# Last projection of the first layer: half of each sum in three f32r terms, half in fp32

## The chip, the cores and the metric

The kernel runs on one core of one Trainium2 chip. The metric is the device time of one execution in microseconds (us); a kernel's time is the median of its runs. Engine names: PE is TensorE, DVE VectorE, ACT ScalarE, POOL GpSimd, SP SyncE.

## The reference, cut to what matters

Two decoder layers over x of shape (2, 1024, 256), each with self-attention, cross-attention and a feed-forward part. The piece around the change is the end of the first layer and the opening of the second:

```
h = gated_gelu(layernorm(x) @ ff_w1 + ff_b1)   # 2048 tokens x 1024
x = x + h @ ff_w2 + ff_b2                      # 1024 -> 256: the projection that is changed
# second layer
h = layernorm(x) * ln1_w + ln1_b
qkv = h @ qkv_w + qkv_b                        # first slices of it are made in the same stage
```

Everything is float32. The projection is a sum over 1024 rows of ff_w2, that is eight row tiles of 128.

## The kernel before

The 2048 tokens are 16 token tiles of 128. `project_norm` (L2591) is one helper for six projections, named po0, pc0, pf0 (first layer) and po1, pc1, pf1 (second). It runs as a block of its own: all engines enter it together and leave it together. The call that changes is pf0 (L3160). Its input `src` is oT (the trace calls it o), 8 row tiles by 2048 tokens, and its weights are w_out (8 row tiles by 256).

**Groups.** The 16 token tiles go in nine groups: seven of two, then two of one (L2595). For group i:

- TensorE `product(i)` (L2727): for each token tile a sum over the KN = 8 row tiles into PSUM. In fp32 each of the eight products appears in the trace as two instructions (two passes). Then `turn(i - 1)` (L2759), four transposes of normalised rows (two in a single-tile group), then the work that `beside` brings along.
- VectorE `stats_of(i)` (L2789): adds the product to x (L2796), takes statistics and the variance plus eps (L2804, L2808, L2811). Then `normalise(i)` (L2813): a reciprocal and one subtract-and-multiply per token tile (L2822), which waits for ScalarE's square root.
- ScalarE `root(i)` (L2855), then `evacuate(i - 1)` (L2860): the turned rows to hT.
- GpSimd `add_bias` (L2682): the bias onto x, four token tiles at a time, in four instructions (L2686).

**Beside pf0.** `thin_attention` (L85) hands over the opening of the second layer's self-attention. SyncE loads its weights. ScalarE's `clear` (L356) fills q_top and k_top in four 2048-wide instructions, behind the root of group 0. In groups 2 to 9, TensorE makes one part of q/k (L290) and one of v (L298) each, ScalarE and VectorE drain the q/k part (L337, L372), and VectorE drains the v part (L382) behind the group's normalising. GpSimd fills v_buf with ones (L694, `gpsimd_early`) right behind the fourth bias addition, and VectorE's first v drain waits for that (`zeroed`, L377). All four bias additions and the memset stand at the head of GpSimd's queue; it has nothing else in this block.

**Products of parts.** Other calls (po0, pc0, pf1) pass `parts=True`. Then group 0 is still made in fp32, and from group 1 on each sum is 24 f32r products: high half of source times high half of weights, high times low, low times high (L2743). ScalarE makes the high halves (w_hi, once; s_hi per token tile, L2877), VectorE the low half of the weights (L2835) and of even token tiles, GpSimd that of odd token tiles (L2655 in both). s_hi and s_lo are rings of RING = 4 token tiles; ScalarE refills a slot when the product that read it is done (L2880 to L2882). Each engine runs `low_parts` or `high_parts` two groups ahead. With parts, GpSimd's queue has another order (L2704): bias 0, low part of group 1, then for i from 0: a bias addition at i = 0, 2 and 4, and the low part of group i + 2.

```
                if parts:
                    add_bias(0)
                    low_parts(1)
                    for i in range(NG):
                        if i % 2 == 0 and i // 2 + 1 < TT // XCHUNK:
                            add_bias(i // 2 + 1)
                        if i + 2 < NG:
                            low_parts(i + 2)
```

`add_bias(c)` ends in `beside.gpsimd(pool, c)`, so the memset follows the bias addition with c = 3, at i = 4. ScalarE, for each i, runs high_parts(i + 2), root(i), evacuate(i - 1), then beside; VectorE stats_of(i), low_parts(i + 2), normalise(i), then beside.

Of the kernel before, what the change touches and what calls it, by code (L numbers as in the profile page):

```python
# [20 lines left out]
F32 = mybir.dt.float32  # L21
F32R = mybir.dt.float32r
BF16 = mybir.dt.bfloat16
U8 = mybir.dt.uint8
ALU = mybir.AluOpType
ACT = mybir.ActivationFunctionType
AX = mybir.AxisListType

P = 128
B, T, D = 2, 1024, 256  # L30
# [2558 lines left out]


def project_norm(nc, shared, name, src, wts, loads, early, x, ln, hT, ident, out, prefetch=(), x_in=None, x_src=None,  # L2591
                 beside=Beside(), split=None, parts=False, lag=1):

    groups, at = [], 0
    for size in [GROUP] * (TT // GROUP - 1) + [1] * GROUP:  # L2595
# [3 lines left out]
    NG = len(groups)  # L2599
    RING = 2 * GROUP  # L2600
# [3 lines left out]
    with ExitStack() as ctx:  # L2604
        def sb(n, shape, dt=F32):
            return ctx.enter_context(nc.sbuf_tensor(f"{name}_{n}", shape, dt))

        KN = src.shape[1] if src is not None else 0
# [6 lines left out]
        hn = sb("normed", [P, 2, GROUP, D]) if ln else None  # L2615
        if parts:

            w_hi, w_lo = [sb(n, [P, KN, D], F32R) for n in ("w_hi", "w_lo")]
            s_hi, s_lo = [sb(n, [P, RING, KN, P], F32R) for n in ("src_hi", "src_lo")]
        prod = [ctx.enter_context(nc.psum_tensor(f"{name}_prod{i}", [P, GROUP, D], F32)) for i in range(NPROD)]  # L2620
        turned = [ctx.enter_context(nc.psum_tensor(f"{name}_turned{i}", [P, KD, GROUP * P], F32)) for i in range(2)]

# [15 lines left out]
        w_high, w_low = shared["w_high"], shared["w_low"]  # L2638
# [13 lines left out]
        def low_part(engine, j):  # L2652

            at = slice(j * P, (j + 1) * P)
            engine.tensor_tensor(s_lo[:, j % RING], src[:, :, at], s_hi[:, j % RING].bitcast(F32),  # L2655
                                 ALU.subtract).then_inc(src_low[j % 2].sem, 1)

        with nc.Block() as block:  # L2658
# [66 lines left out]
            @block.tensor  # L2725
            def _(pe):
                def product(i):  # L2727
                    first, size = groups[i]
                    if i == 0:
                        pe.wait_ge(loaded.sem, loaded.since(DMA * len(loads)))  # L2730
                    if i >= NPROD:
                        pe.wait_ge(summed.sem, summed.since(i - NPROD + 1))
                    for t in range(size):
                        at = (first + t) * P
                        if parts and i:
                            mm = product_of_parts(i, t, first + t)
                            continue
                        for k in range(KN):
                            mm = pe.matmul(prod[i % NPROD][:, t, :], src[:, k, at:at + P], wt[:, k, :],  # L2739
                                           start=(k == 0), stop=(k == KN - 1))  # L2740
                    mm.then_inc(prod_full.sem, 1)

                def product_of_parts(i, t, j):  # L2743
                    dst, u = prod[i % NPROD][:, t, :], j % RING
                    if i == 1 and t == 0:
                        pe.wait_ge(w_high.sem, w_high.since(1))
                    pe.wait_ge(src_high.sem, src_high.since(j - GROUP + 1))
                    for k in range(KN):
                        pe.matmul(dst, s_hi[:, u, k, :], w_hi[:, k, :], start=(k == 0), stop=False)  # L2749
                    if i == 1 and t == 0:  # L2750
                        pe.wait_ge(w_low.sem, w_low.since(1))
                    for k in range(KN):
                        pe.matmul(dst, s_hi[:, u, k, :], w_lo[:, k, :], start=False, stop=False)  # L2753
                    pe.wait_ge(src_low[j % 2].sem, src_low[j % 2].since((j - GROUP) // 2 + 1))
                    for k in range(KN):
                        mm = pe.matmul(dst, s_lo[:, u, k, :], w_hi[:, k, :], start=False, stop=(k == KN - 1))  # L2756
                    return mm

                def turn(i):  # L2759
                    first, size = groups[i]  # L2760
                    pe.wait_ge(normed.sem, normed.since(i + 1))
                    if i >= 2:
                        pe.wait_ge(h_done.sem, h_done.since(i - 1))
                    for k in range(KD):
                        for t in range(size):
                            mm = pe.transpose(turned[i % 2][:, k, t * P:(t + 1) * P],
                                              hn[:, i % 2, t, k * P:(k + 1) * P], ident[:])
                    mm.then_inc(turn_full.sem, 1)

                def ready(i):  # L2770
                    pe.wait_ge(h_done.sem, h_done.since(i + 1))

                for i in range(NG):
                    if KN:
                        beside.source(pe, groups[i][0])
                        product(i)
                    if ln and i >= lag:
                        turn(i - lag)
                    beside.tensor(pe, i, ready)
                if ln:  # L2780
                    for i in range(NG - lag, NG):
                        turn(i)
                    beside.tensor(pe, NG, ready)

            @block.vector
            def _(dve):
# [45 lines left out]
                beside.ahead(dve)  # L2832
                if parts:
                    dve.wait_ge(w_high.sem, w_high.since(1))
                    dve.tensor_tensor(w_lo[:], wt[:], w_hi[:].bitcast(F32), ALU.subtract).then_inc(w_low.sem, 1)  # L2835
                    low_parts(1)
                ahead = lag - 1 if KN else 1
                for i in range(ahead):
# [15 lines left out]
            def _(act):  # L2854
# [22 lines left out]
                def high_parts(i):  # L2877
                    for j in tiles_of(i):
                        at = slice(j * P, (j + 1) * P)
                        if j >= RING + GROUP:  # L2880
                            pe_at = group_of[j - RING] + 1
                            act.wait_ge(prod_full.sem, prod_full.since(pe_at))  # L2882
                        nc.scalar.activation(s_hi[:, j % RING], src[:, :, at],
                                             ACT.Identity).then_inc(src_high.sem, 1)

                if parts:
                    act.wait_ge(loaded.sem, loaded.since(DMA * len(loads)))
                    nc.scalar.activation(w_hi[:], wt[:], ACT.Identity).then_inc(w_high.sem, 1)
                    high_parts(1)
                for i in range(NG if parts and not ln else 0):  # L2890
                    if i + 2 < NG:
# [191 lines left out]
def decoder_blocks(nc, a, out):  # L3083
# [16 lines left out]
    with ExitStack() as ctx, ExitStack() as thin_ctx:  # L3100
# [28 lines left out]
        with scoped("o0", [P, NG, NT]) as oT:  # L3129
            with scoped("w_out0", [P, NG, D]) as w_out, scoped("bias_out0", [P, D]) as bias_out:  # L3130
# [11 lines left out]
                with scoped("wk0", [P, KC, HEADS * 64]) as wk, scoped("wv0", [P, KC, HEADS * 64]) as wv, \  # L3142
                        scoped("wq0", [P, KD, HEADS * 64]) as wq:
                    fetch_kv = [(wk[0:CW], by_rows(L0["ca_wk"], CW), kv_in[0]), (wv[0:CW], by_rows(L0["ca_wv"], CW), kv_in[0]),
                                (wq[:], by_rows(L0["ca_wq"]), kv_in[0])]
                    kv = {"wk": wk, "wv": wv, "wq": wq, "sem": kv_in[0], "count": len(fetch_kv)}
                    project_norm(nc, norm_sems, "po0", oT, wts, loads, True, x, True, hT, ident, None, fetch_kv, x_in, x_dram,
                                 parts=True)
                    loads = norm_loads(wts, [(w_out[:], by_rows(L0["ca_wo"]))], L0["ca_bo"], (L0["ln3_g"], L0["ln3_b"]))
                    folded_attention(nc, "ca0", hT, ctxT, ident, kv, oT, loads)  # L3150
                with ExitStack() as ff_ctx:
                    split, hidden = hidden_layer(nc, "ff0", ff_ctx, by_rows(L0["ff_w1"]), column(L0["ff_b1"]), True)
                    project_norm(nc, norm_sems, "pc0", oT, wts, loads, True, x, True, hT, ident, None, split=split,
                                 parts=True)
                    loads = norm_loads(wts, [(w_out[:], by_rows(L0["ff_w2"]))], L0["ff_b2"], (L1["ln1_w"], L1["ln1_b"]))
                    hidden(oT, loads)
                early, run, finish = thin_attention(nc, "sa1", thin_ctx, hT, ident, key_low, a["causal_rows"],
                                                    {"qkv": by_rows(L1["qkv_w"]), "bias": column(L1["qkv_b"]),
                                                     "bias_row": row(L1["qkv_b"])})
                project_norm(nc, norm_sems, "pf0", oT, wts, loads, True, x, True, hT, ident, None, beside=early)  # L3160

        thin = {"G": 4, "dh": 16, "biased": True}
        NG = HEADS // 4
# [32 lines left out]
        with scoped("w_out2", [P, 4 * D // P, D]) as w_out, scoped("bias_out2", [P, D]) as bias_out, \  # L3196
                scoped("hid1", [P, 4 * D // P, NT]) as hid:
            wts = {"w": w_out, "bias": bias_out, "ln": lns}
            loads = norm_loads(wts, [(w_out[:], by_rows(L1["mlp2_w"]))], L1["mlp2_b"], None)
            hidden(hid, loads)  # L3200
            ff_ctx.close()
            project_norm(nc, norm_sems, "pf1", hid, wts, loads, True, x, False, hT, ident, out_dram, parts=True)


def causal_rows():
# [32 lines left out]
```

## Time and profile before

| | |
|---|---|
| median of 3 runs | 1787.26 us (1785.79 to 1788.02) |
| profiled execution, its own time | 1787.46 us |
| its span, first to last instruction | 1785.7 us |
| PE busy over the span | 1633.4 us, 91% |
| DVE, ACT, POOL busy | 64%, 59%, 54% |
| mean granted TensorE clock | 0.975 |
| the stage pf0 | about 1128.7 to 1210.4 us |

Busy time is that of instructions of one engine, overlaps counted once. The granted clock is the share of TensorE's full 2.4 GHz that the chip gives; it is 1.00 or 0.50, and a number between is a mean over a stretch with both. In a timeline each row is a run of instructions of one kind on one engine, and the idle time in front of them stands in brackets with what ended it; LDWEIGHTS (PEld) overlaps the products. A wait for several things is put down to the one that came last.

### The profile page before, as it was taken

To read this page: it belongs to the slowest core of one execution; us is meant where nothing else is said; L and a number is where in the kernel's file an instruction comes from. 1 tells how busy PE (TensorE), PEld (TensorE's weight loads), DVE (VectorE), ACT (ScalarE), POOL (GpSimd) and SP (SyncE) were. 2 spreads that over 40 slices of the span, in tenths; PEclk is the share of its full clock that TensorE was granted. 3 is DMA by queue.
4 is the path that set the end of the run, shared out by engine and by line. 5 is a ranking of instruction groups with operands and counts; after the bars stand their busy time and mean duration, and the time that the engine had idled before them with its cause. 6 is when DMAs were issued, how large, how long until landed. Compare 5 with 4: busy or idle time off the path is not lost. (4 is left out here: it accounts for less than half of the span.)

```text
span 1785.7 us, 28486 instructions
## 1 busy us (share of the span) xinstructions
PE 1633.4 (91%) x9748; PEld 1046.9 (59%) x9748; DVE 1141.7 (64%) x1985; ACT 1060.8 (59%) x1376; POOL 962.2 (54%) x734
## 2 busy tenths in 40 slices
PE   6889999999999999988998989996989888898799
PEld 4445545444444444378787978884445436565579
DVE  7557677777777777476775933347787845776513
ACT  4556688888888888833556433311767772454452
POOL 1456688888888888952233710202334444566405
PEclk9999999999999999999999999995999999999899
DMA  3011021111111111030000010103234321000101
GB/s 98 24 34 33 36 69 37 43 35 41 53 47 35 41 35 36 24 107 27 1 2 13 1 39 24 25 13 90 55 85 96 73 74 31 9 1 2 36 15 48
DMA packets 54312, 70.92 MB, mean 40 GB/s; under 512 B 18176, under 2 KB 41884, under 8 KB 54207
## 3 DMA queue, kind: packets, MB, share of 16 engines
q1 hardware_dynamic: 54207, 69.54, 14.0%
q8 instruction: 63, 1.03, 0.2%
q14 instruction: 42, 0.34, 0.1%
HBM read 41.72 MB, written 2.37 MB: 25 GB/s over the span
## 5 line engine op out<-in xcount | busy, mean ns | idle before, releaser
L1694 POOL TENSOR_TENSOR x<-x,sa_p_buf 128x1024 f32<-128x1024 f32 x190 | 453.5, 2387 | 126.9 <-ACT sa_p_buf L1430 114.1
L1562 DVE TENSOR_REDUCE sa_mx<-sa_front 128x1 f32<-128x512 f32 x512 | 327.7, 682 | 106.4 <-PE sa_front L1285 105.4
L1430 ACT ACTIVATE sa_p_buf<-sa_score 128x1024 f32<-128x1024 f32 x256 | 249.2, 1023 | 130.6 <-PE sa_score L1322 130.4
L1341 PE MATMUL sa_out<-sa_p_buf,sa_v_buf 128*64 128x512 f32 x1024 | 246.4, 602 | 0.0
L607 ACT ACTIVATE sa_p_buf<-sa_score 128x1024 f32<-128x1024 f32 (+1 forms) x160 | 140.6, 942 | 74.6 <-PE sa_score L555 74.5
L402 DVE TENSOR_REDUCE sa_mx<-sa_front 128x1 f32<-128x512 f32 (+1 forms) x224 | 136.5, 651 | 31.8 <-PE sa_front L316 28.3
L2686 POOL TENSOR_TENSOR x<-x,bias_out 128x1024 f32<-128x1024 f32 x24 | 61.3, 2570 | 168.8 <-POOLq L3014 142.0
L1285 PE MATMUL sa_front<-sa_k_hi,sa_q_hi 64*128 64x512 f32 x512 | 116.8, 452 | 22.2 <-DVE sa_mx L1562 17.1
L1341 PEld LDWEIGHTS sa_out<-sa_p_buf,sa_v_buf 128*64 128x64 f32 x1024 | 64.5, 136 | 123.6 <-issue 97.5
L1440 ACT ACTIVATE sa_score<-sa_m_all 128x1024 f32<-128x1024 f32 x128 | 130.9, 1035 | 0.5 <-DMA sa_m_all<-sa_m_line 0.5
L660 POOL TENSOR_SCALAR_AFFINE_SELECT sa_p_buf<-sa_p_buf 128x128 f32<-128x128 f32 x256 | 65.6, 293 | 119.2 <-ACT sa_p_buf L607 119.2
L1440 ACT ACTIVATE sa_score<-x 128x1024 f32<-128x1024 f32 x128 | 127.6, 1030 | 1.7 <-DMA x<-sa_m_line 1.7
L1285 PEld LDWEIGHTS sa_front<-sa_k_hi,sa_q_hi 64*128 64x128 f32 x512 | 48.2, 184 | 125.6 <-DVE sa_mx L1562 57.7
L1584 DVE RECIPROCAL x<-x 128x128 f32<-128x128 f32 x124 | 108.7, 920 | 17.5 <-ACT x L1453 17.1
L1322 PE MATMUL sa_score<-sa_q_hi,sa_k_hi 64*128 64x512 f32 x512 | 107.9, 418 | 1.9 <-ACT sa_score L1440 1.8
L1322 PE MATMUL sa_score<-sa_q_hi,sa_k_lo 64*128 64x512 f32 x512 | 101.5, 392 | 0.0
L1322 PE MATMUL sa_score<-sa_q_lo,sa_k_hi 64*128 64x512 f32 x512 | 101.3, 392 | 0.0
L316 PE MATMUL sa_front<-sa_k_top,sa_q_top 33*128 33x128 f32 (+4 forms) x504 | 71.2, 349 | 23.0 <-DVE sa_mx L402 14.8
L316 PEld LDWEIGHTS sa_front<-sa_k_top,sa_q_top 33*128 33x128 f32 (+1 forms) x504 | 43.7, 193 | 77.5 <-DVE sa_mx L402 52.1
L3040 PE MATMUL ff_ps<-ff_h_hi,ff_w_hi 128*128 128x512 f32 x192 | 77.5, 404 | 8.2 <-PEq L2658 6.3
L2557 POOL TENSOR_TENSOR wk<-ca_s_sb,ca_inv 128x616 f32<-128x616 f32 x32 | 39.0, 1219 | 82.3 <-DVE ca_inv L2504 81.1
L575 PE MATMUL sa_out<-sa_p_buf,sa_v_buf 128*32 128x512 f32 (+3 forms) x768 | 78.7, 497 | 3.0 <-POOL sa_p_buf L660 3.0
(284 smaller groups left out, 3526.7 us busy)
## 6 DMA issues: line engine op xcount, KB each, us to landing
sa_m_all<-sa_m_line SPq DMA_DIRECT2D x16, 512.0 KB, 3.7
x<-sa_m_line SPq DMA_DIRECT2D x16, 512.0 KB, 4.4
sa_v_buf<-o SPq DMA_DIRECT2D x15, 512.0 KB, 5.1
x<-in_x SPq DMA_DIRECT2D x8, 512.0 KB, 5.5
sa_q_stack<-sa_hi SPq DMA_DIRECT2D x32, 128.0 KB, 2.6
sa_k_stack<-sa_hi SPq DMA_DIRECT2D x32, 128.0 KB, 2.7
sa_recip<-sa_den_out SPq DMA_DIRECT2D x32, 128.0 KB, 2.7
ff_w<-in_L_xattn_ff_w SPq DMA_DIRECT2D x16, 128.0 KB, 2.1
```

The lines of the kernel that those rows point to most:

```text
L316: mm = pe.matmul(bank(i, item, u)[:, c0 + lo_k:c0 + hi_k], q_top[base:base + rows_of, b, r, at], k_top[base:base + rows_of, b, r, k0 + lo_ ...
L402: dve.tensor_reduce(mx[:, b, j, place:place + 1], fr[u][:, 0:n], AX.X, ALU.max).then_inc(drained, 1)
L575: mm = pe.matmul(out_ps[32 * j:32 * j + 32, q0 - h * HALF:q0 - h * HALF + n], v_buf[:, b, kt, at:at + 32], p_buf[:, unit(i, s) % NPB, j, c ...
L607: nc.scalar.activation(p_buf[:, n % NPB, 2 * r:2 * r + 2, 0:cols], score_ps[r][:, :, 0:cols], ACT.Exp, scale=SCALE).then_inc(exp_done, 1)
L1285: pe.matmul(front_ps[bank(item, j)][:], q_hi[r, b, qt * P:(qt + 1) * P], k_hi[r, b, half * HALF:(half + 1) * HALF], start=True, stop=True) ...
L1322: mm = pe.matmul(score_ps[s % len(score_ps)][:, j, :], ks[r, b, keys], qs[r, b, queries], start=False, stop=(part == 2), skip_group_check= ...
L1341: mm = pe.matmul(out_ps[64 * j:64 * j + 64, :], v_buf[:, b, kt, 64 * j:64 * j + 64], p_buf[:, s % NPB, j, :], start=(kt == 0), stop=(kt == ...
L1430: nc.scalar.activation(p_buf[:, s % NPB], score_ps[s % len(score_ps)][:], ACT.Exp, scale=SCALE).then_inc(exp_done, G)
L1440: nc.scalar.activation(score_ps[s % len(score_ps)][:], m_all[h].rearrange("p (j n) -> p j n", j=G), ACT.Identity).then_inc(seeded, G)
L1562: dve.tensor_reduce(mx[:, b, j, qt, half:half + 1], front_ps[bank(item, j)][:], AX.X, ALU.max).then_inc(drained, 1)
L1584: dve.reciprocal(recip[:, h, at], recip[:, h, at]).then_inc(inverted, 1)
L1694: nc.gpsimd.tensor_tensor(acc[:, h], prev, cur, ALU.add).then_inc(added, 1)
```

## The change

`parts` becomes a number of row tiles instead of yes or no. The first `parts` row tiles of a sum are made of three f32r terms, those from `parts` on in fp32, ahead of them in the same sum. The buffers for the halves have `parts` row tiles. po0 and pc0 pass NG (8) and pf1 passes 4 * D // P (8): their KN, so they keep what they had. pf0 passed nothing and now passes 4.

```diff
-                 beside=Beside(), split=None, parts=False, lag=1):
+                 beside=Beside(), split=None, parts=0, lag=1):
...
-            w_hi, w_lo = [sb(n, [P, KN, D], F32R) for n in ("w_hi", "w_lo")]
-            s_hi, s_lo = [sb(n, [P, RING, KN, P], F32R) for n in ("src_hi", "src_lo")]
+            w_hi, w_lo = [sb(n, [P, parts, D], F32R) for n in ("w_hi", "w_lo")]
+            s_hi, s_lo = [sb(n, [P, RING, parts, P], F32R) for n in ("src_hi", "src_lo")]
...
-            engine.tensor_tensor(s_lo[:, j % RING], src[:, :, at], s_hi[:, j % RING].bitcast(F32),
+            engine.tensor_tensor(s_lo[:, j % RING], src[:, 0:parts, at], s_hi[:, j % RING].bitcast(F32),
...
-                    for k in range(KN):
-                        pe.matmul(dst, s_hi[:, u, k, :], w_hi[:, k, :], start=(k == 0), stop=False)
+                    for k in range(parts, KN):
+                        pe.matmul(dst, src[:, k, j * P:(j + 1) * P], wt[:, k, :], start=(k == parts), stop=False)
+                    for k in range(parts):
+                        pe.matmul(dst, s_hi[:, u, k, :], w_hi[:, k, :], start=(k == 0 and parts == KN), stop=False)
...
-                    for k in range(KN):
+                    for k in range(parts):
                         pe.matmul(dst, s_hi[:, u, k, :], w_lo[:, k, :], start=False, stop=False)
...
-                    for k in range(KN):
-                        mm = pe.matmul(dst, s_lo[:, u, k, :], w_hi[:, k, :], start=False, stop=(k == KN - 1))
+                    for k in range(parts):
+                        mm = pe.matmul(dst, s_lo[:, u, k, :], w_hi[:, k, :], start=False, stop=(k == parts - 1))
...
-                    dve.tensor_tensor(w_lo[:], wt[:], w_hi[:].bitcast(F32), ALU.subtract).then_inc(w_low.sem, 1)
+                    dve.tensor_tensor(w_lo[:], wt[:, 0:parts], w_hi[:].bitcast(F32), ALU.subtract).then_inc(w_low.sem, 1)
...
-                        nc.scalar.activation(s_hi[:, j % RING], src[:, :, at],
+                        nc.scalar.activation(s_hi[:, j % RING], src[:, 0:parts, at],
...
-                    nc.scalar.activation(w_hi[:], wt[:], ACT.Identity).then_inc(w_high.sem, 1)
+                    nc.scalar.activation(w_hi[:], wt[:, 0:parts], ACT.Identity).then_inc(w_high.sem, 1)
...
-                project_norm(nc, norm_sems, "pf0", oT, wts, loads, True, x, True, hT, ident, None, beside=early)
+                project_norm(nc, norm_sems, "pf0", oT, wts, loads, True, x, True, hT, ident, None, beside=early, parts=4)
```

## Rows read from the trace of the kernel before

**Rows 1.** Busy time by stretch: us, PE, PEld, DVE, ACT, POOL, clock, DMA, GB/s.

```profile
1155.00:1165.00 10.00, 10.00 (x50) 8.80 (x49) 3.91 (x13) 1.48 (x4) 0.00 (x0) 1.00 0.01 2
```

**Rows 2.** Timeline, a steady group of pf0: start us, us, instructions [idle before].

```profile
1160.68 0.60 PE L2766 MATMUL pf_turned<-ident,pf_normed 128*128 128x128 f32 x4
1160.96 0.69 DVE L2796 TENSOR_TENSOR x<-pf_prod,x 128x512 f32<-128x512 f32 x1 [5.34 <-PE pf_prod L2739]
...
1163.39 0.73 DVE L2822 TENSOR_SCALAR pf_normed<-x,pf_mean_var,pf_inverse 128x256 f32<-128x256 f32 x2
...
1163.71 7.07 PE L2739 MATMUL pf_prod<-w_out,o 128*128 128x256 f32 x32
...
1164.86 0.68 DVE L382 TENSOR_TENSOR sa_v_buf<-pf_front,sa_bv 128x512 f32<-128x512 f32 x1
...
1170.62 0.60 PE L2766 MATMUL pf_turned<-ident,pf_normed 128*128 128x128 f32 x4
...
1171.92 1.89 PE L298 MATMUL pf_front<-sa_wv,hT 128*128 128x256 f32 x8
...
1173.65 7.07 PE L2739 MATMUL pf_prod<-w_out,o 128*128 128x256 f32 x32
```

**Rows 3.** Chain that ended last, start of pf1: start us, us, what.

```profile
1735.61 7.14 PE pf_prod L2739 x32
...
1743.70 0.96 PE pf_prod L2753 x8
```

**Rows 4.** Timeline of PE in pc0, end of a group of f32r products.

```profile
1023.06 1.12 PE L2756 MATMUL pc_prod<-pc_w_hi,pc_src_lo 128*128 128x256 f32 x8
1024.02 0.60 PE L2766 MATMUL pc_turned<-ident,pc_normed 128*128 128x128 f32 x4
```

**Rows 5.** Timeline of all engines, the opening of pf0.

```profile
1128.69 9.28 POOL L2686 TENSOR_TENSOR x<-x,bias_out 128x1024 f32<-128x1024 f32 x4 [91.34 <-POOLq L3014]
1128.71 14.05 PE L2739 MATMUL pf_prod<-w_out,o 128*128 128x256 f32 x64 [1.11 <-PEq L3014]
...
1137.76 4.33 DVE L2811 TENSOR_SCALAR pf_var_eps<-pf_mean_var 128x2 f32<-128x2 f32 x1
1137.91 4.15 POOL L694 MEMSET sa_v_buf<- 128x4864 f32 x1
...
1142.23 1.90 ACT L358 ACTIVATE sa_q_top<-sa_recip 128x2048 fp32r<-128x2048 f32 x1
...
1143.35 0.65 PE L2766 MATMUL pf_turned<-ident,pf_normed 128*128 128x128 f32 x4 [0.59 <-DVE pf_normed L2822]
...
1147.63 1.90 ACT L358 ACTIVATE sa_k_top<-sa_recip 128x2048 fp32r<-128x2048 f32 x1
```

**Rows 6.** Timeline of all engines in pc0: a subtraction, and a copy 512 wide.

```profile
985.94 1.22 DVE L2655 TENSOR_TENSOR pc_src_lo<-o,pc_src_hi 128x1024 fp32r<-128x1024 f32 x1
...
1001.05 0.62 ACT L2875 ACTIVATE ff_h_hi<-hT 128x512 fp32r<-128x512 f32 x1
```

**Rows 7.** Line 2695 alone, subtractions on POOL: duration ns min/median/max, first and last start.

```profile
L2695 POOL TENSOR_TENSOR ff_h_lo<-hT,ff_h_hi x18: 722/1272/1467, 1001.7 to 1684.2; 128x512 fp32r<-128x512 f32 x14, 128x256 fp32r<-128x256 f32 x4
```

**Rows 8.** Timeline of all engines in po0: DVE and POOL at once.

```profile
800.12 3.34 POOL L2655 TENSOR_TENSOR po_src_lo<-o,po_src_hi 128x1024 fp32r<-128x1024 f32 x1 [2.85 <-ACT po_src_hi L2883]
...
801.31 4.68 DVE L2822 TENSOR_SCALAR po_normed<-x,po_mean_var,po_inverse 128x256 f32<-128x256 f32 x2
...
803.42 2.42 POOL L2686 TENSOR_TENSOR x<-x,bias_out 128x1024 f32<-128x1024 f32 x1
```

**Rows 9.** Waits of PE, 760 to 1040 us: us in total, times, longest.

```profile
PE po_prod L2739 <- PEq L1199: 4.5, 1, 4.5
PE ff_ps L3040 <- PEq L2658: 2.8, 1, 2.8
```

**Rows 10.** Busy time by stretch behind these two idle times, columns of rows 1.

```profile
767.30:770.20 2.90, 2.85 (x7) 2.34 (x8) 0.93 (x1) 2.87 (x3) 0.00 (x0) 0.51 0.58 181
1037.70:1043.20 5.50, 5.50 (x13) 4.34 (x14) 0.01 (x1) 1.93 (x2) 0.00 (x0) 0.50 0.75 216
```

More of the change, by code:

```diff
@@ L3147, in decoder_blocks @@
                     project_norm(nc, norm_sems, "po0", oT, wts, loads, True, x, True, hT, ident, None, fetch_kv, x_in, x_dram,
-                                 parts=True)
+                                 parts=NG)
                     loads = norm_loads(wts, [(w_out[:], by_rows(L0["ca_wo"]))], L0["ca_bo"], (L0["ln3_g"], L0["ln3_b"]))
@@ L3153, in decoder_blocks @@
                     project_norm(nc, norm_sems, "pc0", oT, wts, loads, True, x, True, hT, ident, None, split=split,
-                                 parts=True)
+                                 parts=NG)
                     loads = norm_loads(wts, [(w_out[:], by_rows(L0["ff_w2"]))], L0["ff_b2"], (L1["ln1_w"], L1["ln1_b"]))
@@ L3201, in decoder_blocks @@
             ff_ctx.close()
-            project_norm(nc, norm_sems, "pf1", hid, wts, loads, True, x, False, hT, ident, out_dram, parts=True)
+            project_norm(nc, norm_sems, "pf1", hid, wts, loads, True, x, False, hT, ident, out_dram, parts=4 * D // P)
 def causal_rows():
```

## The prediction

> **What bounds the kernel now.** I read first the stretches of the stage that is changed, then its timeline, then the chain of waits, then the other projections, which already do what is added here. The stage (pf0) runs from 1128.7 to about 1210.4 us. In its middle TensorE is busy for 10.00 of 10 us at a granted clock of 1.00, while VectorE has 3.91, ScalarE 1.48 and GpSimd nothing [rows 1]. So what TensorE gives up here shortens the run, and each new wait of TensorE lengthens it.
>
> A steady group of two row tiles of tokens takes 9.94 us on TensorE [rows 2]: 32 passes of the fp32 product, 1163.71 to 1170.62 = 6.91; the turning of the previous group and the first q/k product, 1.30; the v product, 1.73. It is 0.216 us per pass, 0.432 per fp32 product of 128x256.
>
> **Part 1: the product.** Group 0 stays fp32. Fourteen token tiles remain; in each, four fp32 products become twelve of f32r. Eight f32r products take 0.96 us in the chain of waits, 0.120 each [rows 3]. So 4 x 0.432 = 1.73 becomes 12 x 0.120 = 1.44: 0.288 per token tile, 14 x 0.288 = **-4.03 us**. A group of two takes 6.34 instead of 6.91.
>
> The Trainium skill (FP8 and Floating Point Precision, TensorE Precision Notes) says a true fp32 product is four passes. Three would then save a quarter, 0.108 on each 0.432, 6.0 us in all. The trace shows a sixth, since an f32r product here costs 0.120 and not 0.108; the rows decide.
>
> Changing over between forms: from fp32 to f32r the chain of waits shows no gap (7.14 us from 1735.61 end where the f32r pieces, one of which is shown, begin) [rows 3], and the turning follows f32r after one more step, 8 x 0.12 = 0.96 from 1023.06 to 1024.02 [rows 4]. An fp32 product straight behind f32r is shown nowhere; it happens six times (second tile of groups 1 to 6). Bounds: 0, as in these rows, and one f32r step, 0.12 each, 0.7 in all. Less than 0 is excluded, since passes are not skipped. I take 0, the nearest rows.
>
> **Part 2: the opening.** Before, GpSimd did four bias additions (9.28 us) and then the memset of sa_v_buf (4.15); a VectorE instruction of 0.17 lay under it for 4.33, and TensorE waited for the first turning, at 1143.35 [rows 5]. Group 1's product began at 1128.71 + 6.91 = 1135.62 and was through at 1142.53: a wait of 0.82. Now GpSimd has one bias addition, a subtraction, the second addition and a subtraction before about 1138, the memset comes later, and VectorE, with one low part more, has normalised group 0 by about 1140, before product 1 ends at 1135.62 + 6.34 = 1141.96. **-0.82 us**.
>
> New here: ScalarE copies w_hi (twice as wide as the 0.62 row, about 1.2) and four source tiles (0.6 each), VectorE makes w_lo (about 1.2, as the other 1024-wide subtraction), GpSimd subtracts in odd tiles (1.27) [rows 6, 7]. All of it lies under the 6.91 us of group 0, in which ScalarE and VectorE have nothing else. Without that cover it would be some 5 us. No DMA is added or moved; SP's queue is as it was.
>
> **Part 3: the first new wait, at the turning of group 1.** ScalarE must copy the source tiles of group 3 (tiles 6, 7) before it takes the second square root. It gets to them only after the four clears, 1142.23 to 1149.53, 7.3 us [rows 5], which now begin 4.1 us earlier, about 1138.1, and end at 1145.4. The copies are there at 1146.0 and 1146.5; VectorE subtracts until 1146.7; GpSimd starts on tile 7 then (to 1148.0) and goes on at once with the third bias addition (2.35, to 1150.3). VectorE's normalising is two instructions. In po0 the same pair, begun at 801.31 behind GpSimd's 800.12 to 803.46 and 803.42 to 805.84, took 4.68 us and ended at 805.99, after both [rows 8]; alone it takes 0.73 [rows 2]. So group 1 is normalised at about 1150.5. TensorE is through with group 2 at 1135.62 + 6.34 + 0.44 + 6.34 = 1148.74 (the turning is 1.30 less two fp32 products of q/k, 0.44). Wait: **+1.7 us**. The other end is 0, if the second instruction slips in between. I take 1.7, since the row is the same pair behind the same two kinds of work.
>
> The Trainium skill (SBUF — State Buffer, Who interferes with whom) says whichever of VectorE and GpSimd begins first keeps their shared port for its whole instruction. The trace agrees, 4.68 against 0.73; by that rule the term is 1.7, without it 0.
>
> **Part 4: the second new wait, which I expect to decide.** VectorE's drain of the first v product waits for the memset. GpSimd used to do that at the start. Now it stands behind the fourth bias addition, and that behind the low part of tile 11, whose source copy goes into a ring of four and waits until product 3 has read its slot. Queued behind the waiting drain on VectorE are the sum, statistics and normalising of group 3, and TensorE's turning of group 3 waits for these. ScalarE's root of group 3 and what follows it wait with it.
>
> From the end E of product 3 on TensorE: visible to the others at E + 0.28 (the turning starts at 1160.68, the sum that waits for the product at 1160.96 [rows 2]); ScalarE copies tiles 10 and 11, 1.1 -> 1.4; GpSimd's low part 1.27 -> 2.7; bias addition 2.35 -> 5.0; memset 4.15 -> 9.2 [rows 5, 6, 7]; VectorE's drain 0.68 -> 9.9; from the start of the sum to the end of normalising 1160.96 to 1164.12 = 3.16, with one low part of about 0.6 in between -> 13.7 [rows 2]. Meanwhile TensorE has the turning and q/k, v products, 1.30 + 1.73, and product 4, 6.34: 9.37. That is 4.3; in these rows a few instructions start up to 0.1 before the one ahead has ended, so I take **+4.1 us**. Bounds: eight handovers, each 0.1 shorter or 0.05 longer than in a plain sum, 3.5 and 4.7. Less is excluded by the order of the queues, as long as VectorE waits for the memset. Afterwards a group needs VectorE for 3.91 us as in [rows 1] and a low part of 0.6, under 5 of 9.4, so no third wait is due, and the tail (single tiles) only gets shorter.
>
> **Part 5: the clock.** A TensorE idle for 4.1 us may come back at 1.2 GHz. After 4.5 us idle before po0 the granted clock was 0.51 for 2.90 us; after 2.8 us idle before the feed-forward part, at 1037.70, it was 0.50 for 5.50 [rows 9, 10]. Half the work of such a stretch is lost: 1.4 or 2.75. Zero is the lower end, if the clock stays up. I take 1.4, from the row with the nearest idle time: **+1.4 us**. The shorter wait of Part 3 I cost at nothing here.
>
> **Sum:** -4.03 - 0.82 + 1.7 + 4.1 + 1.4 = +2.35. The profiled execution took 1787.46 us (span 1785.7 and 1.76 around it), 0.2 above the median of three runs, 1787.26. So 1789.8 us.
>
> **Rivals.**
> 1. The clock stays up. Sum +0.95: 1788.4. For it: no row shows an idle time of just this length. Against: both idle stretches shown, 2.8 and 4.5, came back at half clock [rows 9, 10].
> 2. The waits do not appear: TensorE is still the bound and the gain lands whole. -4.03 - 0.82 = -4.85: 1782.6. For it: TensorE has no slack and every helper has. Against: the order of GpSimd's queue; it needs the chain of Part 4 to be 4.1 us shorter, which is the whole memset.
> 3. Slower: the low clock lasts as in the longer row. Behind the wait at the turning of group 3, TensorE works 5.5 us at half clock instead of 2.9. +0.95 + 2.75 = +3.7: 1791.2. It decides from about 4.9 us at half clock on, since 1790.8 is +3.4. For it: the 5.50 us row. Against: the row with the nearest idle time has 2.90.
> 4. The change does nothing: the f32r products cost what fp32 does. Against: 0.120 and 0.216 are plain [rows 2, 3]. The calls po0, pc0 and pf1 pass 8, their row tiles, po1 and pc1 pass nothing, so all five keep their instructions. Its time: 4.0 more than the forecast, 1793.8.
>
> **How the numbers follow.** About 0.2%, 3.6 us, is what a measurement of this kernel can tell from no change. Forecast 0.50 (own range 1788.5 to 1790.8); rival 1 0.18; rival 2 0.09; rivals 3 and 4 0.23. Within 0.2% are the forecast and rival 1, 0.68; faster 0.09; slower 0.23. The low end: no wait in Part 3 and no lost clock give -4.03 - 0.82 + 4.1 = -0.75, 1786.7, less half a microsecond for product and run-to-run: 1786.0. The high end takes in rival 3 and the upper bounds of the wait (0.6) and of the six changes of form (0.7): 1792.5.
>
> **What would show it.** Product groups of 6.34 us; pf_src_lo on GpSimd and VectorE at 512 wide; the memset after the fourth bias addition, starting some 5 us after product 3; a VectorE wait of about 14 us ended by the memset, in front of the first v drain; a turning of group 3 with about 4 us idle before it and one of group 1 with 1.7; the granted clock 0.5 behind the first of these. Wrong would be: GpSimd done with the memset before product 3, a turning that never waits, or a third wait.

## The result, and the profile after

The changed kernel took **1795.61 us** (median of six runs, 1793.19 to 1808.33) against 1786.98 for the kernel before (six runs): ratio 1.0053, 95% interval 1.0033 to 1.0072. That is slower, and outside the range given (1786.0 to 1792.5). The profiled execution took 1797.62 us, span 1795.9, mean granted clock 0.970 (before 0.975).

First the changed stage, timeline of the changed kernel: start us, us, instructions [idle before].

```profile
1141.90 0.60 PE L2768 MATMUL pf_turned<-ident,pf_normed 128*128 128x128 f32 x4
...
1146.64 3.57 DVE L2824 TENSOR_SCALAR pf_normed<-x,pf_mean_var,pf_inverse 128x256 f32<-128x256 f32 x2
1147.64 2.42 POOL L2686 TENSOR_TENSOR x<-x,bias_out 128x1024 f32<-128x1024 f32 x1
...
1150.27 0.65 PE L2768 MATMUL pf_turned<-ident,pf_normed 128*128 128x128 f32 x4 [1.46 <-DVE pf_normed L2824]
...
1164.61 4.15 POOL L694 MEMSET sa_v_buf<- 128x4864 f32 x1
1168.85 0.69 DVE L382 TENSOR_TENSOR sa_v_buf<-pf_front,sa_bv 128x512 f32<-128x512 f32 x1 [14.74 <-POOL sa_v_buf L694]
...
1172.91 1.11 PE L2768 MATMUL pf_turned<-ident,pf_normed 128*128 128x128 f32 x4 [3.75 <-DVE pf_normed L2824]
...
1186.97 1.89 PE L2749 MATMUL pf_prod<-w_out,o 128*128 128x256 f32 x8
...
1193.28 0.60 PE L2768 MATMUL pf_turned<-ident,pf_normed 128*128 128x128 f32 x4
...
1196.31 1.89 PE L2749 MATMUL pf_prod<-w_out,o 128*128 128x256 f32 x8
```

A group's product takes 1193.28 - 1186.97 = 6.31 us (before 6.91, [rows 2]) and a group 9.34 (before 9.94). The first turning no longer waits. The two predicted waits are there, at the turnings of group 1 (1.46) and of group 3 (3.75), behind the causes named: normalising drawn out beside GpSimd, and VectorE held for 14.74 us by the memset. The clock is low for 3.4 us behind the second (to 1176.3). The stage, counted from its first product to the first product of the attention block, went from 82.90 to 85.34 us, **+2.44**.

So 8 of the 10 us by which the span grew came elsewhere. The attention block behind the stage took 269.44 us before and 277.30 after, **+7.9**; the other stages differ by under 2 us each and cancel. Nearly all of it lies in one place. Both kernels open the block with 37.5 us at half clock (from 1213.9 before, from 1217.3 after); what differs comes later. Busy time by stretch, the changed kernel (columns of [rows 1]):

```profile
1302.00:1306.00 4.00, 2.57 (x25) 1.09 (x21) 3.21 (x8) 1.94 (x2) 1.11 (x4) 1.00 0.20 33
1306.00:1310.00 4.00, 4.00 (x26) 2.11 (x26) 2.13 (x5) 1.94 (x2) 1.76 (x8) 0.50 0.05 10
...
1318.00:1322.00 4.00, 4.00 (x22) 2.62 (x24) 1.02 (x2) 1.93 (x5) 0.76 (x2) 0.50 0.50 132
1322.00:1326.00 4.00, 4.00 (x28) 1.78 (x30) 2.69 (x5) 1.84 (x5) 2.00 (x8) 0.87 0.00 0
```

The kernel before, the same work:

```profile
1299.70:1303.70 4.00, 3.42 (x37) 2.07 (x41) 3.24 (x11) 2.32 (x3) 1.11 (x4) 1.00 0.01 1
1303.70:1307.70 4.00, 3.41 (x36) 1.56 (x38) 3.77 (x6) 2.23 (x4) 3.00 (x12) 1.00 0.43 117
```

Before, the granted clock is 1.00 there. After, it is 0.50 (1.2 GHz) for 17.1 us from 1306.0 on. Just ahead of it stands a stretch in which TensorE is busy for 2.57 of 4 us. The gap in it, in the timeline of the changed kernel:

```profile
1303.82 0.66 PE L316 MATMUL sa_front<-sa_k_top,sa_q_top 33*128 33x128 f32 x8 [1.20 <-DMA sa_q_top<-sa_hi]
```

and in the kernel before:

```profile
1299.88 0.66 PE L316 MATMUL sa_front<-sa_k_top,sa_q_top 33*128 33x128 f32 x8 [0.41 <-DVE sa_mx L402]
```

TensorE waits for the last of eight loads (keys and queries for the row maxima), which SyncE issues one after another. SyncE's queue in the changed kernel:

```profile
1297.92 0.59 SPq L442 DMA_DIRECT2D sa_q_top<-sa_hi  x1
1298.56 1.47 SPq L442 DMA_DIRECT2D sa_k_top<-sa_hi  x1
1300.06 0.59 SPq L442 DMA_DIRECT2D sa_q_top<-sa_hi  x1
```

One issue took 1.47 us instead of 0.59. From 1298.5 to 1300.0 the DMA queues of the changed kernel show, beside these loads, one transfer of another kind:

```profile
q8 instruction: 1, 0.02, 3.8%
```

This is a fetch of 16 KB of TensorE's instruction stream. That it is TensorE's is read from how often it comes: in the kernel before, the 20 such fetches from 1105.8 to 1482.4 us stand 257 of TensorE's instructions apart on average (178 to 328), which makes 64 bytes for each. Before, the nearest ones fall at 1290.4 and 1304.1, ahead of these loads (1292.9 to 1297.9) and behind them. The change makes that stream 119 instructions longer: per token tile four fp32 products (each two weight loads and two passes) become twelve of f32r (each one and one), 14 x 8 = 112, and 7 waits. So every fetch behind the stage falls on other work, and one whole fetch more, 256 instructions, would bring them back to the same work.

That is a chain of four links (longer stream, late issue, wait, half clock) read from one execution. The experiments test them.

### The profile page after: what moved, and what is told of

It reads as the page before. It is cut to its first block and busy times, and to the rows that moved or that the text cites. A ratio compares the mean times of both kernels' runs of the same rounds, so it can differ in the third digit from the quotient of the medians.

```text
span 1795.9 us, 28635 instructions
## 1 busy us (share of the span) xinstructions
PE 1639.2 (91%) x9804; PEld 1051.4 (59%) x9804; DVE 1146.5 (64%) x1993; ACT 1069.5 (60%) x1391; POOL 971.8 (54%) x741
## 3 DMA queue, kind: packets, MB, share of 16 engines
q1 hardware_dynamic: 54207, 69.54, 13.7%
## 5 line engine op out<-in xcount | busy, mean ns | idle before, releaser
L607 ACT ACTIVATE sa_p_buf<-sa_score 128x1024 f32<-128x1024 f32 (+1 forms) x160 | 140.5, 942 | 79.4 <-PE sa_score L555 79.3
L1285 PE MATMUL sa_front<-sa_k_hi,sa_q_hi 64*128 64x512 f32 x512 | 117.2, 453 | 22.2 <-DVE sa_mx L1562 17.1
L1584 DVE RECIPROCAL x<-x 128x128 f32<-128x128 f32 x124 | 108.7, 920 | 17.5 <-ACT x L1453 17.1
```

Source lines behind the costliest of these rows:

```text
L607: nc.scalar.activation(p_buf[:, n % NPB, 2 * r:2 * r + 2, 0:cols], score_ps[r][:, :, 0:cols], ACT.Exp, scale=SCALE).then_inc(exp_done, 1)
L1285: pe.matmul(front_ps[bank(item, j)][:], q_hi[r, b, qt * P:(qt + 1) * P], k_hi[r, b, half * HALF:(half + 1) * HALF], start=True, stop=True) ...
L1584: dve.reciprocal(recip[:, h, at], recip[:, h, at]).then_inc(inverted, 1)
```

## The experiments

Three sessions, each timed against the kernel before in the same session: 1788.78, 1788.31 and 1788.11 us. The changed kernel itself was timed only in the six runs above, so a difference from it is best read as the difference of the two excesses over before. "Block" is the attention block of the profiled execution (before 269.44, after 277.30), "stage" the projection (82.90, 85.34). Each is of one execution, but the blocks fall apart clearly: in the 14 profiles eight took 269.4 to 270.5 us and six 272.5 to 277.3. The whole time of one profiled execution tells less, since the stages ahead of pf0, to which no edit adds work, took 1125.7 to 1131.8 us.

**1. Is it enough that the block starts later?** The kernel before, with three idle products in group 4:

```diff
+if name == "pf0" and i == 4:
+    for n in range(3):
+        pe.matmul(prod[i % NPROD][:]..., src[:, n, ...],
+                  wt[:, 0:2, :]..., ...)
```

> The kernel before, with three more fp32 products of 128x512 in front of group 4 of pf0: about 2.6 us more for TensorE and only 12 more TensorE instructions. Theory 1 (the next block loses time because it starts some 2.3 us later than before): the attention block behind pf0 grows from 269.4 us to about 277 and the run takes 1795 to 1797. Theory 2 (it loses time because TensorE's instruction stream is 119 instructions longer, so that its fetches fall on other work): the block stays near 269.4 and the run takes 1789 to 1790.

1790.95 us, ratio 1.0017 (1.0007 to 1.0026); stage 85.46, block 269.85, with the clock at 1.00 from the end of the opening 37.5 us on. The block starts 2.9 us later than before, and only 0.4 us is lost in it: a later start is not the cause. The time is 1 us above the 1789 to 1790 that theory 2 gave; it is 2.2 us over before, and the added work makes the stage alone 2.6 longer.

**2. Is it the length of the stream?** Waits on semaphores long past their values, added ahead of each token tile, nine in the kernel before, nine or ten in the changed one:

```diff
+if name == "pf0" and i:
+    for n in NORM_SEMS[:9 - ((first + t) in ())]:
+        pe.wait_ge(shared[n].sem, shared[n].since(0))
```

In the changed kernel the second line is

```diff
+    for n in NORM_SEMS[:10 - ((first + t) in (2, 3, 4))]:
```

> The kernel before, with 118 TensorE instructions more in pf0 that only wait for semaphores already reached, about nine at each token tile. The changed kernel has 119 more. TensorE is 8 of 10 us in its products there, so pf0 should keep its length. Theory 1: 1787, attention block 269. Theory 2: the fetches of the instruction stream in the attention block fall as in the changed kernel, less the 2.3 us; the block takes 273 to 277 and the run 1791 to 1795.

> The changed kernel, with 137 more waiting instructions in pf0, so that TensorE's stream is 256 longer than before, which is one fetch of 16 KB if an instruction has 64 bytes. Theory 2: the fetches fall on the same work of the attention block as before, the block is back at about 269.4 and the run takes 1789 to 1790. Theory 1: block 277, run 1795 to 1796.

The streams came out only 62 and 188 instructions longer than that of before (the 126 waits of the first became 62 instructions, about two to one), not as long as meant, and what was expected of one whole fetch more was not tried by them. The first: 1788.56 us, 0.9995 (0.9985 to 1.0005), no slower than before, where theory 2 gave 1791 to 1795. Its profiled execution was the slowest of its ten runs, with a block of 274.62: 13.7 us of low clock at 1444.4, behind no late load and no wait of TensorE over 0.65 us in the 14 us ahead of it, so the clock can fall in this block in another way too. The second: 1793.76 us, 1.0033 (1.0016 to 1.0050), block 272.49; its late issue (1.75) fell in the seventh group of heads, with a wait of 1.48 and 3.4 us of low clock.

Then the lengths that were wanted, with 17 waits at each tile (118 more), and with 19 instructions more at a second place (256 more than before in all):

```diff
+if name == "pf0" and i:
+    for n in NORM_SEMS[:17]:
+        pe.wait_ge(shared[n].sem, shared[n].since(0))
...
+if name == "pf0" and j in (4, 5, 6, 7, 8, 9):
+    for n in NORM_SEMS[:6]:
+        pe.wait_ge(shared[n].sem, shared[n].since(0))
```

> The kernel before with 118 more instructions in TensorE's stream during this projection (waits on semaphores that are long past their values, spread over the fourteen token tiles of the groups behind the first); the change makes the stream 119 longer. No work is added. Theory A (the longer stream moves TensorE's instruction fetches within the attention block behind it, and with them the late issues of SyncE and the fall of the granted clock): in the profile a fetch falls on SyncE's loads of the largest keys and queries near 1296 us, TensorE waits some 1.2 us for them, the clock falls to 0.50 for about 17 us, the attention block takes some 276 us instead of 269.4; over the runs the time is 4 to 7 us above before. Theory B (it is the two new waits and the half clock inside the projection that disturb the block behind it, the length of the stream is nothing): attention block 269.4 us, time within 0.5 us of before.

1792.41 us, 1.0027 (1.0016 to 1.0038): **+4.1 with no work added**. Stage 83.32, block 276.83. The collision came one group of heads earlier than expected. SyncE, then TensorE, then the stretches:

```profile
1261.90 1.66 SPq L442 DMA_DIRECT2D sa_k_top<-sa_hi  x1
```

```profile
1267.35 0.66 PE L316 MATMUL sa_front<-sa_k_top,sa_q_top 33*128 33x128 f32 x8 [1.41 <-DMA sa_q_top<-sa_hi]
```

```profile
1264.00:1268.00 4.00, 2.59 (x28) 1.22 (x30) 2.80 (x8) 2.88 (x4) 0.81 (x3) 1.00 0.41 66
...
1272.00:1284.00 12.00, 11.64 (x64) 5.34 (x62) 7.20 (x12) 4.54 (x7) 4.10 (x16) 0.50 0.51 129
```

Again a late issue, a wait of 1.41, a stretch of 2.59 in 4, and 17.1 us at half clock. The next group of heads has a second wait for the same kind of load, with all eight issues at 0.59 and the clock at 1.00 behind it:

```profile
1304.60 0.66 PE L316 MATMUL sa_front<-sa_k_top,sa_q_top 33*128 33x128 f32 x8 [1.18 <-DMA sa_q_top<-sa_hi]
```

A fetch begins here at 1302.01, just behind the last issue (over at 1301.86), and that load lands 2.66 us after the end of its issue, where the last loads of groups without a fetch near need 1.7 to 1.8. So a fetch goes with a late landing of a load that is already issued, too. Run before_pad has the same: fetch at 1269.18, landing after 2.54, a wait of 1.07, no fall.

> The changed kernel with 137 more of the same empty waits in TensorE's stream, so that it is 256 instructions longer than before: one whole fetch of 16 KB more, and the fetches behind the projection fall on the same instructions as in the kernel before. Theory A: the attention block goes back to 269 to 270 us without the fall of the clock near 1306 us, and what stays is the projection's own +2.4 us: about 1791, 4 us under the changed kernel. Theory B: attention block 276 to 278 us as in the changed kernel, 1795 or a little more.

1790.84 us, 1.0015 (1.0006 to 1.0024): the changed kernel with **more** instructions gives back 4.8 us (1795.61 to 1790.84). Against the before of its own session it is 2.5 us over, where the changed kernel was 8.6 over, and the two intervals do not touch. Block 269.89, stage 85.22. Theory A expected about 1791. The fetches are where it wanted them: counted from the block's start, those of before come at 46.3, 65.2, 78.8 and 92.5 us, here at 46.8, 65.8, 79.3 and 93.0, and in the changed kernel at 36.1, 54.8, 70.2 and 84.8.

**3. Is it the late load itself?** The kernel before, stream untouched, with two tiny loads ahead of the fifth of the eight:

```diff
+if i == 4:
+    eng.wait_ge(late_in, DMA * 2)
 for j in range(G):
     ...
+    for n in range(2 if (i, j) == (3, 2) else 0):
+        eng.dma_start(spare[:, n], bv[0:16, 0:4]).then_inc(late_in, DMA)
```

> The kernel before with two more tiny loads (16 x 4 numbers) that SyncE issues in the attention block ahead of the fifth of the eight loads of the fourth group of heads, near 1295 us: its last loads are issued 1.2 us later, as a fetch made them in the changed kernel. The projection and TensorE's stream are those of before. Theory A (the late issue is what costs): TensorE waits 1 to 1.3 us near 1301 us for the last load, and the granted clock falls to 0.50 for up to 17 us: attention block 272 to 277 us, time 3 to 7 us above before. Theory C (the clock falls for another reason, the late issue only stands beside it): TensorE waits 1.2 us, the clock stays at 1.00, attention block at most 270.7 us.

1791.10 us, 1.0021 (1.0010 to 1.0031); stage 82.88, block 273.70.

```profile
1301.57 0.66 PE L317 MATMUL sa_front<-sa_k_top,sa_q_top 33*128 33x128 f32 x8 [1.61 <-DMA sa_q_top<-sa_hi]
```

```profile
1299.00:1303.00 4.00, 2.39 (x26) 1.19 (x22) 2.69 (x8) 1.94 (x2) 1.11 (x4) 1.00 0.33 53
1303.00:1307.00 4.00, 3.83 (x29) 2.32 (x25) 2.59 (x6) 1.94 (x2) 0.97 (x4) 0.53 0.02 3
1307.00:1313.00 6.00, 5.66 (x34) 2.77 (x32) 2.99 (x6) 1.09 (x2) 2.06 (x9) 0.50 0.52 135
```

No fetch is needed (none falls between 1287.1 and 1310.5): loads 1.2 us late are enough for the wait and for 10.2 us of low clock. This is the link from the issue to the clock, by itself. The eight runs agree: mean clocks of 0.970 to 0.973, against 0.973 to 0.977 in the 27 of before.

**4. Can the loads be given room?** They read only the high half of the queries and keys, but waited for the low half too:

```diff
-rows_split(eng, i)
+eng.wait_ge(hi_done, NPROJ * (i + 1))
```

> The kernel before, with SyncE's loads of the largest keys and queries waiting for ScalarE's high half (which is all that they read) instead of GpSimd's low half, so that they are issued about 1.2 us earlier. Theory A (the attention block is at the margin there, and a late issue of these loads tips the clock): in the profile the loads of the fourth group start near 1291.8 us instead of 1292.9, the clock stays at 1.00 at that place, the attention block takes 269 to 270 us as in the undisturbed kernel before, and the runs give 0 to 1 us less than before. Theory C (the loads do not matter): nothing moves, within 0.5 us of before.

> The changed kernel with the same one wait altered, its TensorE stream as long as in the changed kernel. Theory A: where a fetch falls on these loads their issue is still late, but they have 1.2 us to spare; no wait of TensorE over 0.5 us on them, the attention block 269.5 to 271 us, what stays is the projection's own +2.4 us: 1790 to 1791.5. Theory C: attention block 276 us, about 1795.

On the kernel before: 1789.35 us, 1.0005 (0.9996 to 1.0013), block 269.39: nothing to mend and nothing gained, so this run does not tell the theories apart. On the changed kernel: **1790.51 us**, 1.0015 (1.0006 to 1.0023), block 270.08. The profiled execution is the case one would wish for, since the fetch falls on the same group of loads:

```profile
1300.17 1.42 SPq L442 DMA_DIRECT2D sa_k_top<-sa_hi  x1
```

```profile
1304.55 0.67 PE L316 MATMUL sa_front<-sa_k_top,sa_q_top 33*128 33x128 f32 x8 [0.41 <-DVE sa_mx L402]
```

```profile
1302.00:1306.00 4.00, 3.59 (x34) 1.46 (x32) 3.63 (x11) 3.08 (x4) 0.61 (x3) 1.00 0.24 37
1306.00:1310.00 4.00, 3.61 (x37) 2.01 (x33) 3.10 (x8) 1.96 (x3) 1.83 (x8) 1.00 0.02 3
1310.00:1322.00 12.00, 10.88 (x99) 6.00 (x98) 9.21 (x17) 7.98 (x13) 6.82 (x24) 1.00 0.65 178
```

The issue is drawn out as in the changed kernel, the wait is 0.41 and VectorE's, as in the kernel before, and the clock stays at 1.00.

**5. The predicted wait, and a version that beats both.** The memset at the head of GpSimd's queue:

```diff
-        if step == TT // XCHUNK - 1:
+        if step < 0:
             pool.memset(v_buf[:], 1.0).then_inc(zeroed, 1)
...
+beside.gpsimd(pool, -1)
```

> The changed kernel with the memset of v_buf put at the head of GpSimd's queue, ahead of the first bias addition. The wait at the turning of group 3 (3.75 us) and the half clock behind it (about 1.6) go; the wait at the turning of group 1 stays. pf0 should end 3.2 us before that of the kernel before, near 1207.3 us. If the attention block takes 269.4 the run is 1783.8, if it takes 277 it is 1791.5; both theories allow either, since both start and stream differ.

1790.81 us, 1.0012 (0.9997 to 1.0028). Stage 80.50: the wait of 3.75 and its half clock are gone, 4.84 less than after and 2.4 less than before, while the wait at the turning of group 1 grew to 2.23. The block, with the same stream as the changed kernel, had 17.1 us of half clock again at the same place in it (276.19), behind a wait of 1.21. Not every execution has it: of the ten runs three took 1785.8 to 1787.4 us, the others 1790.7 to 1798.9 at lower mean clocks (0.967 to 0.972 against 0.973 to 0.975).

> The changed kernel with the memset of the values' buffer at the head of GpSimd's queue and the same 137 empty waits. Theory A: the projection gives its -2.4 us (as with the memset alone), the attention block stays at 269 to 270 us, and the time is 2 to 3 us under before: the version that beats both. Theory B: as with the memset alone, attention block 276 us, about 1791.

> The changed kernel with the memset at the head of GpSimd's queue and that one wait altered. Theory A: projection 80.5 us (-2.4), attention block 269.5 to 271 us, time 2 to 3 us under before and 4 us under the memset alone. Theory C: as with the memset alone, attention block 276 us, about 1791.

The first adds the 137 empty waits to the memset at the head, the second the altered wait of experiment 4. They took 1786.65 us, 0.9991 (0.9981 to 1.0000), and 1787.19 us, 0.9996 (0.9986 to 1.0006). Blocks 269.80 and 269.75, as expected; but both stages took 82.02 instead of 80.5, since the clock was low for 3.4 us behind the wait at the turning of group 1, which was as long (2.2) as with the memset alone, where the clock stayed up. So the medians are 0.9 and 1.7 us under before where 2 to 3 were expected, and neither is clear of noise.

Last, in this projection, GpSimd makes the low part ahead of the bias addition:

```diff
+if name == "pf0" and i + 2 < NG:
+    low_parts(i + 2)
 if i % 2 == 0 and i // 2 + 1 < TT // XCHUNK:
     add_bias(i // 2 + 1)
-if i + 2 < NG:
+if name != "pf0" and i + 2 < NG:
     low_parts(i + 2)
```

> The same, and in this projection GpSimd makes the low parts of a group ahead of the addition of the bias instead of behind it. Theory A with the wait at the turning of group 1 put down to the third addition of the bias (as predicted): that wait of 1.46 us goes, the projection takes 79 us, and the time is 1 to 1.5 us under the kernel without this edit. Rival (the low part and the second normalising instruction meet anyway): the wait stays or moves to another turning, projection 80.5 us, no difference.

**1783.68 us, 0.9976 (0.9964 to 0.9988)**: faster than both kernels, 0.24% under before, and the interval stays clear of 1. Stage 79.66, block 270.54. The normalising of group 1 took 3.56 us in the kernel of the run before:

```profile
1148.89 3.56 DVE L2826 TENSOR_SCALAR pf_normed<-x,pf_mean_var,pf_inverse 128x256 f32<-128x256 f32 x2
```

and here

```profile
1146.52 1.14 ACT L2889 ACTIVATE pf_src_hi<-o 128x512 fp32r<-128x512 f32 x2
1147.17 0.69 DVE L2655 TENSOR_TENSOR pf_src_lo<-o,pf_src_hi 128x512 fp32r<-128x512 f32 x1 [3.67 <-ACT pf_src_hi L2889]
...
1147.99 1.49 DVE L2828 TENSOR_SCALAR pf_normed<-x,pf_mean_var,pf_inverse 128x256 f32<-128x256 f32 x2
...
1149.53 0.66 PE L2772 MATMUL pf_turned<-ident,pf_normed 128*128 128x128 f32 x4 [1.39 <-DVE pf_normed L2828]
```

Without the bias addition beside it the pair is 2.07 us shorter, but the wait goes from 2.24 only to 1.39. The rows put what is left down to ScalarE's source copy, which comes only after its four clears (it starts at 1146.52) and for which VectorE waits 3.67; no run moved the clears. Neither side of the expectation was right as put. The stage is 2.36 us shorter than in the run before: 0.85 by the wait and the rest by the clock, which stays up in it. The other 1.1 us between the medians (1787.19, 1783.68) is not accounted for.

## Why the prediction was wrong

By its own steps, from the profile of the changed kernel:

- **Part 1, the product**: 6.31 per group against 6.34 forecast; right, and so is the choice of 0.120 per f32r product. No gap shows where fp32 follows f32r. By the four passes that the Trainium skill (FP8 and Floating Point Precision, TensorE Precision Notes) gives for true fp32, a group would take 6.05, an estimate; the trace does not bear that out.
- **Part 2, the opening**: right, the first turning does not wait.
- **Part 3**: 1.46 against 1.7, by the mechanism named; run first_high_swap shows that taking the bias addition away removes only part of such a wait (0.85 of 2.24).
- **Part 4**: 3.75 against 4.1, by the mechanism named; memset_first takes it away and the stage becomes 4.84 us shorter.
- **Part 5**: 3.4 us at half clock against 2.9; 1.7 lost against 1.4.
- **The sum for the stage**: +2.44 against +2.35. That the sum is this close is in part chance, since errors cancel: the waits came out 0.6 shorter by their brackets, the product saved about 4.2 instead of 4.03, and the dearer clock (+0.3) and small delays at the waits and at the stage's end make up for them. The low end of the range does not follow from its own working (1786.7 less a half is 1786.2, not 1786.0), which decides nothing. With the block undisturbed (after_256, after_high) the whole run is 2.5 and 2.4 us over before, 1790.8 and 1790.5: this is the forecast, 1789.8 and the 1 us by which these sessions' before was above that of the forecast.

**The step that failed is the one that has no term**: it ended the sum at the end of the stage and took the block behind it as unchanged. "No DMA is added or moved" is wrong for the one kind of DMA that no line of the kernel issues. The change adds 119 instructions to TensorE's stream and so moves its fetches. In the changed kernel one falls on eight loads whose last TensorE takes up after waiting 0.41 us for VectorE; an issue 0.88 late (1.47 for 0.59) made the wait 0.79 longer, so they have 0.1 to spare. At that point the wait of 1.20 was followed by 17.1 us at half clock, and the block took 7.9 us more. Shown by themselves: the stream's length (before_118, after_256), the late load (sync_late), and the room that makes it harmless (after_high). Rival 3, the slower one, had the wrong place: low clock, but behind the turning, and 1791.2. Rival 4's 1793.8 lay nearest to the measured time by luck: its ground, that f32r products save nothing, is refuted by the 6.31.

What stays open is what makes the clock fall. At this point of a group of heads, in the kernels whose loads have no extra room, waits of 1.20, 1.21, 1.41, 1.48 and 1.61 us were followed by 17.1, 17.1, 17.1, 3.4 and 10.2 us of half clock (after, memset_first, before_118, after_pad, sync_late), and six waits of 0.86 to 1.18 by none (among them 0.94 in the changed kernel, behind an issue of 1.25 at 1268.81). The length of the low stretch does not follow from the wait, one fall stands behind no such wait (before_pad), and in the stage a wait of 2.2 was followed by a fall in two profiles and by none in a third.

How often the loss comes isn't known either. Three of the kernels whose loads are hit by fetches spread more from run to run (standard deviation 2.5 us in before_118, 4.2 in after_pad, 3.8 in memset_first, against 1.6 to 2.2 in before and 1.6 in after_256 and after_high), so the +4.1 of before_118 is an average over runs of which the profile shows one. The six runs of the changed kernel all lie above the slowest of the six of before (1793.19 against 1790.03), at mean clocks of 0.970 to 0.973 and one of 0.927; how long the clock was low in each, and what made the last so slow (1808.33), no trace shows. Why an issue of SyncE is drawn out by a fetch is not shown; that the two go together is.

## What to carry to other kernels

Where an edit changes how many instructions an engine runs, the stages behind it are not untouched: look for loads there that are issued one by one, land just in time and are taken up by a tightly fed TensorE, and price a microsecond's delay of them, clock included (here 4.3 to 7.9 us on the block in four profiles, for waits 0.8 to 1.8 longer in sum). Give such loads room (let them wait for exactly what they read) before tuning anything ahead of them, or the next edit's gain or loss is not its own. And work that only one late consumer needs, as the memset here, belongs at the head of a helper's queue if that queue will get waits in front of it.

## What the runs showed of the hardware

- Fetches of TensorE's instructions (16 KB on a queue of their own) go with drawn-out issues of SyncE. In the attention block of the 14 profiles 68 of some 3460 issues took 0.92 to 1.98 us in place of 0.59, and each of the 68 has such a fetch beginning within 0.6 us of its own start. The kernel before has them too (0.98 us at 1277.31, fetch at 1276.8), at most places with no effect on TensorE.
- A fetch that began at the end of the issue of a group's last load went with a landing 2.2 to 2.7 us after that issue instead of 1.7 to 1.8 (five cases, two of them in before_118).
- Waits on semaphores that are long past cost TensorE next to nothing: 118 instructions more lengthened the stage by 83.32 - 82.90 = 0.42 us, 4 ns each. The other 3.7 of the 4.1 us went with where they put the fetches.
- Five waits of 1.20 to 1.61 us amid the block's products were each followed by 3.4 to 17.1 us at half the clock, six of 0.86 to 1.18 by none. With one such fall in the block it took 7.9, 7.4, 6.8 and 4.3 us more than before (after, before_118, memset_first, sync_late).
